# A two-layer transformer block on one core: zero products at the start, GpSimd instructions undivided, the last step of every norm on ScalarE

## What is computed

```python
x = x + L0_xattn(layernorm(x), ctx, ctx, mask, ...)   # 16 heads of 8, softmax over 154 context rows
x = x + L0_ffn(layernorm(x), ...)                     # 8 experts 128 -> 512 -> 128, top 2 routed, gelu
x = x + L1_xattn(layernorm(x), ctx, ...)              # self attention, norm, cross attention, norm, feed, norm
x = x + L1_ffn(layernorm(x), ...)                     # 32 experts of 64, top 6 of 4 groups, one shared, silu

def layernorm(x, eps=1e-5):
    return (x - mean(x)) / sqrt(var(x) + eps)         # inside L1_xattn: eps 1e-3, then * gamma + beta
```

## Time and profile before

| | |
|---|---|
| median of 3 runs | 582.1 us (580.37 to 582.15) |
| profiled execution, whole | 581.68 us |
| its span on the core | 579.9 us |
| granted TensorE clock, mean | 0.996 |
| activation table loads | 37 |
| written to and read from HBM | 1.38 MB and 36.45 MB |

### The profile page before, as it was taken

One profiled execution on the slowest core, in us unless ns is written; L12 is line 12 of the kernel. 1 busy time (PEld: TensorE's weight loads), 2 busy tenths in 40 slices (PEclk: granted clock), 3 DMA queues, 4 the chain that ended last, 5 costly groups with the idle time before them and its releaser, 6 DMA issues.

```text
span 579.9 us, 8752 instructions
## 1 busy us (share of the span) xinstructions
PE 554.4 (96%) x2629; PEld 389.6 (67%) x2629; DVE 446.9 (77%) x1343; ACT 378.5 (65%) x663; POOL 190.8 (33%) x265
## 2 busy tenths in 40 slices
PE   4899999999999999999999999999999999999996
PEld 3566566655777677667767677667566766776885
DVE  6898999882454566879577796978988999889774
ACT  2587677757767797757875599865664623565653
POOL 3102020011433112443133413448341011477765
PEclk9999999999999999999999999999999999999998
DMA  4401000301111111003101102441121432432440
GB/s 142 176 20 29 1 9 2 121 25 42 42 47 36 47 37 37 20 18 93 36 20 45 39 19 74 141 110 62 67 90 42 145 92 77 143 114 67 149 151 20
DMA packets 23327, 38.40 MB, mean 66 GB/s; under 512 B 3792, under 2 KB 9552, under 8 KB 22896
## 3 DMA queue, kind: packets, MB, share of 16 engines
q1 hardware_dynamic: 22848, 37.44, 20.6%
q10 hardware_dynamic: 432, 0.40, 0.2%
HBM read 36.45 MB, written 1.38 MB: 65 GB/s over the span
## 4 chain that ended last, share of the span: by engine, by line
PE 72%; DVE 12%; POOL 6%; ACT 4%; issue 4%; DMA 1%; POOLq 0%; DVEq 0%; ACTq 0%
PE ps L1647 9%; PE ps L1649 8%; PE ps L1648 8%; PE ps L1854 7%; PE ps L2027 4%; PE ps L1730 3%; PE ps L1659 3%; PE ps L1660 3%; PE ps L1661 3%; PE ps L1654 3%; PE ps L1750 3%; PE ps L1764 2%; PE ps L1642 2%; PE ps L1767 2%; POOL w1s L790 2%
## 5 line engine op out<-in xcount | busy, mean ns | idle before, releaser
L1647 PE MATMUL ps<-xThi,w1s 128*128 128x512 f32 x256 | 122.8, 480 | 3.0 <-DVE h L1598 1.5
L1006 ACT ACTIVATE h<-ps,early 128x512 f32<-128x512 f32 x128 | 86.2, 686 | 54.8 <-PE ps L1649 48.4
L1649 PE MATMUL ps<-xTlo,w1s 128*128 128x512 f32 x256 | 100.8, 394 | 0.0
L1648 PE MATMUL ps<-xThi,w1s 128*128 128x512 f32 x256 | 100.4, 392 | 0.0
L1137 ACT ACTIVATE s<-ps 128x512 f32<-128x512 f32 x68 | 40.7, 599 | 57.4 <-PE ps L1649 55.7
L790 POOL TENSOR_TENSOR acc_o<-acc_o,ty 128x256 f32<-128x256 f32 x64 | 52.2, 836 | 76.9 <-DVE ty L1398 76.1
L1359 DVE TENSOR_TENSOR h_r<-h,s_r 128x512 fp32r<-128x512 f32 x64 | 48.9, 766 | 26.2 <-ACT s_r L892 26.0
L1854 PE MATMUL ps<-h,w2s 128*128 128x512 f32 x128 | 66.1, 598 | 2.6 <-DVE ty L1398 2.6
L1647 PEld LDWEIGHTS ps<-xThi,w1s 128*128 128x128 f32 x256 | 48.2, 188 | 29.4 <-DVE h L1598 9.0
L790 POOL TENSOR_TENSOR h_r<-h,WB_r 128x256 fp32r<-128x256 f32 x68 | 54.3, 823 | 31.4 <-ACT WB_r L892 31.3
L1302 DVE TENSOR_REDUCE NM<-ps 128x2 f32<-128x308 f32 x128 | 56.6, 472 | 9.5 <-PE ps L1730 7.9
(11 more groups left out here) (291 smaller groups left out, 1150.9 us busy)
## 6 DMA issues: line engine op xcount, KB each, us to landing
CB<-ct_rows SPq DMA_DIRECT2D x128, 128.0 KB, 2.9
WB<-wt_rows SPq DMA_DIRECT2D x32, 256.0 KB, 3.2
w2s<-w_dram SPq DMA_DIRECT2D x2, 2048.0 KB, 9.7
raw<-gu_dram SPq DMA_DIRECT2D x4, 512.0 KB, 4.2
x_in<-x_dram SPq DMA_DIRECT2D x4, 256.0 KB, 3.2
w2s<-dn_dram SPq DMA_DIRECT2D x1, 1024.0 KB, 7.2
out_dram<-ty SPq DMA_DIRECT2D x3, 256.0 KB, 3.0
late<-late_dram SPq DMA_DIRECT2D x1, 608.5 KB, 8.6
```

Source lines behind the costliest of these rows:

```text
L1006: nc.scalar.activation(h32[:, c % HR, :], bank[c % 2], ACT.Gelu, bias=b1T[:, c:c + 1]).then_inc(b_gelu.sem, 1)
L1647: M(dst, w[0], xThi[:, x, :], start=start, stop=False)
L1648: M(dst, w[1], xThi[:, x, :], start=False, stop=False)
L1649: return M(dst, w[0], xTlo[:, x, :], start=False, stop=stop)
```

## The change

- PE gets a new first stage, `idle_turns`: 24 products of a 128x128 corner of WT with itself into PSUM bank 4, which nobody reads. The first waits for WT's memset (`pads`), which moves to the head of DVE's order. PE's wait for `early_loaded` moves from the top into the first `context_keys`, `context_values` and `inputs`.
- `Norm.vector` ends with one more small operation, `-mean * rstd` for the four tiles; the last step becomes `Norm.scalar`: four activations Identity per norm with scale `rstd` and bias `-mean * rstd`, each with its own due time in PLAN_ACT.
- `in_pieces` is gone; every GpSimd operation that was cut is one instruction.
- All five plans are new. PLAN_PE ends at 56014, PLAN_SP's last store stands at 56126.

```diff
 PLAN_ACT = {
-    "warm_up": [[0, 18]],
+    "warm_up": [[0, 1060]],
...
+    "norm_a": [[809, 837, 866, 894], [2134, 2162, 2190, 2270], [4556, 4584, 4714, 4866], [7964, 7992, 8020, 8048]],
...
 PLAN_DVE = {
-    "paddings": [[558, 8109, 9079]],
+    "paddings": [[0, 3151, 5005]],
...
 PLAN_PE = {
-    "context_keys": [[832], [1613], [4765], [7798]],
-    "context_values": [[719], [4315], [7124], [9993]],
-    "inputs": [[921, 1096], [2371, 2850], [5051, 5726], [8182, 8491]],
+    "idle_turns": [[75, 142, 187, 232, 277, 322, 366, 411, 456, 501, 546, 590, 635, 680, 1228, 1251, 1326, 1348, 1370,
+        1393, 1462, 1484, 1758, 1794]],
+    "context_keys": [[779], [1584], [4642], [7708]],
+    "context_values": [[720], [4203], [7080], [10007]],
+    "inputs": [[936, 1074], [2335, 2826], [4950, 5709], [8123, 8250]],
...
@@ class Norm
-            self.t = sb(name + "_t", [P, 4, NT])
-            self.steps = sig(name + "_steps", 2 * NT + 4)
+            self.t = sb(name + "_t", [P, 5, NT])
+            self.steps = sig(name + "_steps", 2 * NT + 5)
...
-            for i in range(NT):
-                if i == 2:
-                    yield
-                nc.vector.tensor_scalar(dst[:, i, :], src[:, i, :], self.mv[:, i, 0:1], t[:, 3, i:i + 1],
-                                        ALU.subtract, ALU.mult).then_inc(self.out.sem, 1)
+            nc.vector.scalar_tensor_tensor(t[:, 4, :], self.mv[:, :, 0], -1.0, t[:, 3, :], ALU.mult, ALU.mult).then_inc(n.sem, 1)
+
+        def scalar(self, eng, b, src, dst):
+
+            for i in range(NT):
+                yield
+                eng.wait_ge(self.steps.sem, self.steps.at(b, 2 * NT + 5))
+                nc.scalar.activation(dst[:, i, :], src[:, i, :], ACT.Identity, bias=self.t[:, 4, i:i + 1],
+                                     scale=self.t[:, 3, i:i + 1]).then_inc(self.out.sem, 1)
...
-                in_pieces(S, h32r[:, t % HR, :], h32[:, t % HR, :], hh1[:, t % 2, :].bitcast(F32), ALU.subtract).then_inc(d_lo.sem, 1)
+                nc.gpsimd.tensor_tensor(h32r[:, t % HR, :], h32[:, t % HR, :], hh1[:, t % 2, :].bitcast(F32), ALU.subtract).then_inc(d_lo.sem, 1)
...
-                in_pieces(S, acc_o[:], acc_o[:], ty[:, e % 2, :], ALU.add).then_inc(b_acc.sem, 1)
+                nc.gpsimd.tensor_tensor(acc_o[:], acc_o[:], ty[:, e % 2, :], ALU.add).then_inc(b_acc.sem, 1)
...
+    NIDLE = 24
...
+        def idle_turns():
+
+            for n in range(NIDLE):
+                yield
+                if not n:
+                    pe.wait_ge(pads.sem, 1)
+                claim(4)
+                M(bank[4][:, 0:P], WT[:, 0, 0:P], WT[:, 0, 0:P], start=True, stop=True)
+                read_by(4, pads, 1)
...
-        pe.wait_ge(early_loaded.sem, 32)
-        merged(PLAN_PE, ("context_keys", map(context_keys, every)), ("context_values", map(context_values, every)),
+        merged(PLAN_PE, ("idle_turns", [idle_turns()]), ("context_keys", map(context_keys, every)), ("context_values", map(context_values, every)),
```

More of the change, by code:

```diff
@@ new lines @@
+    "prepare_b": [[10649, 11506, 12812], [15006, 15705, 18491], [19818, 20611, 24385], [26755, 27755, 30908]],
+    "first": [[12694, 13157, 13447, 13700, 13769, 13996, 14133, 14202, 14359, 14428, 14720, 14789, 15049, 15118, 15410,
[8 rows of a table added]
+    "weights": [[13299], [19304], [26123], [33412]],
+    "second": [[13522, 13841, 13910, 14064, 14273, 14497, 14566, 14652, 14861, 15187, 15255, 15341, 15551, 15864,
[8 rows of a table added]
+    "stage_c": [[14959, 18079, 18847, 19390, 19574, 19660], [25794, 26077, 26301, 26387], [32454, 32668, 32852, 32938]
+        , [38699, 39657, 39844, 39930]],
@@ L785, in _ @@
     def _(pool):
-        def in_pieces(n, out, a, b, op, width=256):
-            for c in range(0, n, width):
-                q = slice(c, min(c + width, n))
-                last = nc.gpsimd.tensor_tensor(out[:, q], a[:, q], b[:, q], op)
-            return last
         def constants():
@@ L820, in split2 @@
                 pool.wait_ge(w2_hi.sem, w2_hi.at(0, k + 1))
-                for c in range(8 * k, 8 * k + 8, 2):
-                    hi = w2h[:, c * P:(c + 2) * P].bitcast(F32).rearrange("p (c k) -> p c k", k=P)
-                    last = nc.gpsimd.tensor_tensor(odd_low[:, c:c + 2, :], odd[:, c:c + 2, :], hi, ALU.subtract)
-                last.then_inc(w2_lo.sem, 1)
+                o, c = slice(8 * k, 8 * k + 8), slice(1024 * k, 1024 * k + 1024)
+                nc.gpsimd.tensor_tensor(odd_low[:, o, :], odd[:, o, :], w2h[:, c].bitcast(F32).rearrange("p (c k) -> p c k", k=P),
+                                        ALU.subtract).then_inc(w2_lo.sem, 1)
         def split3():
@@ L830, in split3 @@
                 w, hi, low = down1_piece(k)
-                in_pieces(512 if k else P, low, w, hi.bitcast(F32), ALU.subtract).then_inc(dn_lo.sem, 1)
+                nc.gpsimd.tensor_tensor(low, w, hi.bitcast(F32), ALU.subtract).then_inc(dn_lo.sem, 1)
         def lows_d(b):
@@ L876, in stage_c @@
                 pool.wait_ge(c_a3.sem, c_a3.at(b, 0))
-            for i in range(0, NT, 2):
-                last = nc.gpsimd.tensor_tensor(norm2b[:, i:i + 2, :], norm2[:, i:i + 2, :], over_tiles(rows["b2f"], 2), ALU.add)
-            last.then_inc(c_n2b.sem, 1)
+            nc.gpsimd.tensor_tensor(norm2b[:], norm2[:], over_tiles(rows["b2f"]), ALU.add).then_inc(c_n2b.sem, 1)
             yield from ln_n3.gpsimd(pool, b)
@@ L1209, in normalised @@
                 dve.wait_ge(a_qn.sem, a_qn.at(b, 0))
-            yield from ln_a.vector(dve, b, x_in, xn)
+            yield from ln_a.vector(dve, b, x_in)
         def keys(b):
@@ L1345, in norm_b @@
                 dve.wait_ge(b_xT_ps.sem, b_xT_ps.at(b, 0))
-            yield from ln_b.vector(dve, b, X2[:, b, :, :], xn2)
+            yield from ln_b.vector(dve, b, X2[:, b, :, :])
         def halves_b(b):
@@ L1412, in norm_c @@
             dve.wait_ge(b_x2.sem, b_x2.at(b, 1))
-            yield from ln_c.vector(dve, b, X2[:, b, :, :], xi)
+            yield from ln_c.vector(dve, b, X2[:, b, :, :])
         def maxima_c(b):
@@ L1449, in self_out @@
             dve.wait_ge(c_att.sem, c_att.at(b, 2))
-            yield from ln_n1.vector(dve, b, a1, normed)
+            yield from ln_n1.vector(dve, b, a1)
             yield
@@ L1481, in feed @@
             dve.wait_ge(c_a2.sem, c_a2.at(b, 1))
-            yield from ln_n2.vector(dve, b, a1, normed)
+            yield from ln_n2.vector(dve, b, a1)
             yield
@@ L1497, in feed @@
             dve.wait_ge(c_a3.sem, c_a3.at(b, 1))
-            yield from ln_n3.vector(dve, b, a1, normed)
+            yield from ln_n3.vector(dve, b, a1)
             yield
@@ L1513, in norm_d @@
                 dve.wait_ge(b_xT_ps.sem, b_xT_ps.at(NB, 0))
-            yield from ln_d.vector(dve, b, X2[:, b, :, :], xn2)
+            yield from ln_d.vector(dve, b, X2[:, b, :, :])
         def halves_d(b):
@@ L1676, in context_values @@
             yield
+            if not b:
+                pe.wait_ge(early_loaded.sem, 32)
             pe.wait_ge(a_ctx_in.sem, a_ctx_in.at(b, 32))
```

276 lines of the change are left out of this document (144 added, 132 removed), and 197 rows, old and new, of tables (PLAN_ACT, PLAN_DVE, PLAN_PE, PLAN_SP).

## The result

The changed kernel takes 583.23 us (median of 11 runs, 582.94 to 583.56), the kernel before 581.27 us (11 runs, 580.23 to 582.54): a ratio of 1.0036 [1.0026, 1.0045]. By the medians it is slower by 2.0 us, where 579.8 us had been forecast, 2.3 us under the 582.1 us of the first three runs.

A forecast was written before the change was run, and what follows sets the result against it. PE, busy 554.4 of 579.9 us, was taken as the bound, through idle time and slow-clock products. Clock -2.9, rest of first norm +0.45, order +0.5, GpSimd -0.3 sum to -2.25 us: 579.8 us forecast, range 576.2 to 584.2.

The forecast's parts named there:

- Part 1, the clock: PE's start: zero products raise the clock early and speed up the first real products; -2.9 us, bounds 2.0 and 4.0.
- Rival B: PE's start: the clock does not rise early, or falls again; 583.7 us, chance 0.16.
- the lead: PE after the start: the clock's 2.9 us gain is kept; if gone at 128 us or later, the order sets the end.
- Part 2, the norms: 28 norms' last step: DVE loses 34 us, ACT gains 41, hidden except in the first norm, +0.6 us.
- Part 2, the length: ACT's 112 last-step activations of 128x128 with two columns: 0.37 us each, bounds 0.27 and 0.47.
- 0.27 to 0.47 named as a sign: ACT's Identity instruction in the norms: its length in us should stand in this range.
- Rival C: ACT's queue: each norm holds ACT and lets 0.2 us through to PE, 5.6 us in all; 585.4 us, chance 0.12.
- Part 4, the order: All plans' due times: the ends of PE's plan and SP's last store move later; +0.5 us, give or take 2.
- Part 3, GpSimd undivided: POOL's 512-column operations: 1.27 us each; the last two `h_r` give -0.3 us, bounds 0 and -1; port wait free on the path.
- The mean of the DVE line that should have risen to 0.9: DVE line L1604, two SBUF inputs: its mean should rise from 0.82 towards 0.9 us as POOL's instructions lengthen.
- D, DVE's relief: PE's 6.6 us of waits for DVE and POOL: half goes as DVE is relieved; 576.5 us, chance 0.14.
- the 413 to 425 forecast: DVE's busy time over the run: should come to between 413 and 425 us.

The follow-up runs named there:

- e1: The kernel before, in its old order, with the 24 zero products alone: 579.23 us, ratio 0.9963.
- x3: The changed kernel with the norms' last step on ScalarE as a plain copy, scale and bias left out: 574.24 us, ratio 0.9875.
- c2: The changed kernel with the norms' last step as a copy with the scale column but no bias column: 577.21 us, ratio 0.9920.
- e3: The kernel before, in its old order, with all seven norms' last step on ScalarE and nothing else: 607.92 us, ratio 1.0455.
- n4: The changed kernel, in its new order, with all norms' last step back on VectorE: 583.93 us, ratio 1.0043.
- c1: The changed kernel with the last step still Identity with two columns, but both the constant -0.5: 583.21 us, ratio 1.0029.
- n1: The new order with none of the three parts (norms on VectorE, GpSimd cut, no zero products): 590.01 us, ratio 1.0145.
- e2: The kernel before, in its old order, with GpSimd's operations undivided and nothing else: 584.26 us, ratio 1.0049.
- x2: e1 with the new order's sequence from a due time of 45000 on, GpSimd in pieces: 588.9 us, ratio 1.0125.
- x1: n4 with the old order's sequence from a due time of 45000 on: 582.04 us, ratio 1.0008.
- h3: The changed kernel with one of each norm's four tiles on DVE and the old sequence from due time 45000 on: 580.92 us, ratio 0.9977.
- h4: The changed kernel with two of each norm's four tiles on DVE and the old sequence from due time 45000 on: 579.92 us, ratio 0.9965.

## Why the prediction was wrong

The time of 583.23 us lies inside the stated range, 576.2 to 584.2, but a gain of 2.3 us was forecast and a loss of 2.0 us measured.

- *Part 1, the clock, -2.9 us.* Right in place and nearly in size: -2.4 us at 31 us, -2.7 at 160; alone (e1) it measured -2.1, or 0.37% of the time, in either order. The bounds were 2.0 and 4.0. The 14 turns ran from 1.97 to 7.46 us (1.7 to 7.7 forecast) and nothing was late for them. Rival B fell; the transposes among the early work did not stop the clock from holding. (They are not most of it, as rival B has it: 20 of the 48 records from 6 to 22 us in the kernel before.) That it rose so early and held is what the eight records at 1.06 and 1.16 us show.
- *"PE is the busiest engine behind it, so the lead should be kept."* True in e1, false in the changed kernel, where it was gone by 324 us. As the forecast said, that the lead would be there at 25 us and gone later means that the order, and not the clock, sets the end, but "the order" turned out to be only half of the cause.
- *Part 2, the norms: here is the step that failed*, its cover: *"ACT gains 41 us and comes to 420 of 580. That is no bound, and elsewhere than in the first norm PE's other work hides it."* ACT came to 416.9, and the work did not hide it: PE's waits for ScalarE went from 3.5 to 7.0 us. I put 27 of the 28 norms at nothing. x3 against the changed kernel takes 28 x 0.74 = 21 us off ScalarE and 1.6% or 9 us off the whole, so 45% of the step's length beyond a copy's came through; its second column alone is worth 6.7 us (c2). The norms on ScalarE in an order not made for them (e3) cost 26 us. A share of busy time over the whole run said nothing of a queue in which gelus, silus and copies stand close behind the steps. What n4 adds is that the norms on DVE fare no better in this order: the cover was missing there too.
- *Part 2, the length*, was nearly right. The 0.37 us were a price with the overlap of neighbours taken off, and start to start the steps stand 0.386 us apart. Without the overlap the same working gives 0.47 us, and one took 0.484, just outside the 0.27 to 0.47 named as a sign. The rows it was built on read PSUM, where the copy takes 0.267 us; x3's copy reads SBUF and takes 0.300. The Trainium skill, "ScalarE: Activation LUTs", in What ACT_TABLE_LOAD costs, gives 186 ns and 0.833 ns a column without pointer operands and about 93 ns for each such operand: 293, 386 and 479 ns for 128 columns, which x3, c2 and c1 bear out with 300, 391 and 484 ns. The first norm came out near the forecast: from the small step's start to the end of the fourth, 1.84 us for 1.74.
- *Rival C* was the right mechanism, at the right place, with a chance of 0.12: it asked for 0.2 us a norm. By x3 it is 0.32 us a norm beyond a copy's length. My sum for it began at the forecast's 579.8, which had taken the order at +0.5; the order with a short step is 7.3 us faster than before, so 574.0 + 9 gives the 583.2 measured.
- *Part 4, the order, +0.5 +-2 us.* Far off in both directions, and not a number of its own. Without the parts the new order is 1.45% slower than the old one (n1), with them and a step shorter than its slot 1.25% faster (x3). The diff shows the slots: the entries of one norm stand mostly 28 apart in PLAN_ACT, 0.28 us, against my own price of 0.37 us, overlap already taken off, and 0.386 measured. My own numbers had the step overrun its slot by 0.09 us. I used due times for the sum, but never set a slot beside the price of what stands in it.
- *Part 3, GpSimd undivided, -0.3 us and no cost from the port.* `h_r` of 512 columns took 1.421 us in the mean: the 6 that meet no DVE operation with two SBUF inputs take 1.28 us, as forecast (1.27), the 28 that do 1.45. The mean of the DVE line that should have risen to 0.9 fell from 0.823 to 0.812 us. Each meeting did get longer, 0.92 before and 0.96 us after where a GpSimd instruction is at work (up to 1.57), 0.69 where none is; but 29 of the 64 meet one, where 37 did. Single places show more: 2.45 us for 0.81 in e2 and 1.26 for 0.16 at 318 us. It is 0.49% alone in the old order, and a gain of 0.30% in the new one.
- *D, DVE's relief.* DVE lost 26.4 us, busy 420.5, within the 413 to 425 forecast, and that was luck: I had 34 less 7 for the port. The 34 added up the lengths of instructions that overlap (38 us; their busy time before is 32.8), and the 7 did not come. From 390 to 536 us DVE fell to 82%, and PE did not profit. PE's wait for the maxima did shrink, from 1.7 to 0.7 us. Instead DVE itself waited longer for ScalarE's silu, 5.6 us over the run where it had been 2.4 (3.7 in x3), nearly all of it in that stretch, and PE for DVE's `h`, 2.3 for 1.5 us. The number of table loads stayed at 37.

Shown: the clock's part; that the step's length, and not the data, makes 1.6% of the time; that sharing the step out brings 0.7% back; that PE's waits for ScalarE rise and fall with the length. Shown in part: through what the delay reaches PE. The 128 gelus of stage B start 131 us in sum after the end of their products in the kernel after, 116 in x3 and 109 before; the 15 that stand right behind a norm's step have 4.6 of the 15 us, so most of it travels down the queue to later entries. In stage D DVE's longer waits for the silu point the same way. Open: why the stretch from 441 to 528 us is slower in every kernel with a part of the new order. It costs 4.8 us in the kernel after, 3 in x3 and 9.2 in x2, and with the old sequence behind 45000 still 3.0 in x1, 3.7 in h3 and 2.8 in h4, but only 0.2 in e1. Exchanging that sequence gave back 1.8 us in x1 and nothing in h3. Not tried: an order searched anew with the step at 0.39 us.

## What to carry to other kernels

Where an order is made from due times, set each slot beside the measured length of what stands in it; a step that overruns its slot by 0.1 us at 96 places cost 1.2% here, on an engine that was idle for 28% of the run. Price each variant of an instruction by its operands (none, one or two columns), from a row that reads the same memory. A part's worth belongs to the order it stands in: GpSimd's long operations cost 0.49% in one and gained 0.30% in the other. Work can be shared between two engines instead of moved: one tile of four on DVE beat none, two and four, and that share was found by trying it: by the slots alone it would have been two tiles on DVE, which leave ScalarE 0.97 us of work in 1.14 us.

## What the hardware showed that I had not expected

- Each column operand (a scale or bias read from SBUF, one value per row) costs an activation 0.09 us: 0.300, 0.391 and 0.484 us for 128 columns with none, one and two, and neighbours overlap by 0.09 to 0.1 us (four of 0.484 in 1.65).
- A DVE operation on 128x4 elements was held up for 1.1 us, to the end of a POOL addition that had begun 0.03 us before it. The Trainium skill, "SBUF — State Buffer", in Who interferes with whom, says that a DVE instruction with two SBUF inputs contends with a GpSimd instruction that reads SBUF, and of the shared pair of ports that the later of the two fully blocks; the trace agrees at this place, and adds that even the smallest operations can pay the full price. It is rare: 5 of the 160 DVE operations of 128x4 in the kernel after took over 0.4 us.
- At the end of the run the clock stayed at 1.00 from 575 to 578 us, where it had been 0.52 before, with PE busy 1.85 us in the 3 us ahead of it instead of 1.53.
